# A state-space layer and a mixture of experts in one kernel: a scan started from zero, earlier weight scales, and group 0's pieces placed anew

## The chip, the cores and the metric

The kernel runs on one core of a Trainium2 chip. Its engines are PE (TensorE, matrix products; its weight loads are PEld), DVE (VectorE), ACT (ScalarE), POOL (GpSimd) and SP, which issues the DMA transfers. Each engine runs its own list of instructions in order, and they wait for each other through semaphores. The metric is the time of one execution on the device in microseconds (us); shorter is better. Times inside an execution are in us from its first instruction.

## The reference

Two layers, each followed by a residual and a layer norm, on x of 2 x 2048 tokens with 256 features. Cut to what matters:

```python
# layer 1: a recurrence over time, 128 states
xB = einsum('bsd,nd->bsn', x, B)
state = tanh(state @ A.T + xb_t)              # one token after another, from zero
out = states @ C.T + D * x
x = layernorm(x + layernorm(out + x) * gamma + beta)
# layer 2: 8 experts, 2 chosen per token, and a shared one
scores = sigmoid(x @ router_weight.T)
# the better of two groups of 4 experts by the sum of its top two, then the top two in it
comb = chosen scores / their sum
y = sum_e comb[:, e] * (silu(x @ w_gate[e]) * (x @ w_up[e])) @ w_down[e]
x = layernorm(x + y + (silu(x @ sw_gate) * (x @ sw_up)) @ sw_down)
```

## The kernel before

**Tiling.** The 4096 tokens are 128 runs of L = 32 consecutive tokens, one run on each partition. Tile l is the l-th token of all runs. x is loaded in eight chunks of four tiles (chunk 7 first, then 0 to 6), transposed on PE in 32 halves (`turn_x`), and kept in xT.

**The scan** treats the 128 runs side by side, so that one step is one tile: PE adds the product of x (`drive`, L295) and of the state before (L301), ACT takes the tanh (L526). A run's first state is the last of the run in front of it, which isn't known at first. So there are three stretches: WARM = 4 steps on the last four tiles from zero, whose end gives the seeds; pass one, 32 steps from these seeds; and pass two, 32 steps from pass one's ends, whose states are kept. Afterwards the check compares pass two's ends with the seeds it started from (L822 to L831). Where they differ by more than 2^-20, all engines take a branch that runs the recurrence token by token and does group 0 again (`again`). Between the steps stand the turns of x, those of C and the router's weights, and two small PE instructions for the weight scales.

**Scales and splits.** Every weight tensor is split into two f16 parts for PE. DVE takes each one's largest absolute value (L635); PE transposes the five maxima (L322), DVE reduces them and puts them on a diagonal (L641, L643), PE spreads them over all partitions (L326), and DVE forms powers of two from them (`scales`, L645 to L660). `split(i)` makes the high part (L666) and the low part (L668) of one tensor: 0 is wg, 1 wu, 2 the router's weights rw, 3 wd, 4 C.

**POOL** adds 1 to D, then computes eight times `skip` (x times D, L941), eight times `residual` (x plus beta, L949), the last two behind the two `rsqrt` of group 0 (L961, L963), and later a difference per expert (L978).

**Group 0's pieces.** Tokens then go through eight groups of four tiles. For a group the nine `piece(e, ...)` of PE, ACT and DVE make what the experts need: e = 0 and 1 the product with C (L344, which needs the buffer that DVE's L709 reads), layer norms on DVE (L694 to L734), e = 4 and 5 the transposition of x2 (L359), e = 6 the router's product (L370), e = 7 the tanh of the routing scores (L516), then `choose` and `weigh` on DVE (L759 to L805). Group 0's pieces stand inside pass two, at the steps that the tables `PE_AT` and `ACT_AT` name: `{10: (1, 0)}` puts the first half of piece 1 behind step 10. From step `UP_FROM` on, two of the 24 products of experts 0 and 1 (`early_up`, L382) follow each step, the rest follow the scan. Then comes the check, and then the transposition of group 0's weights (`turn_comb(0)`, L446), with which the groups begin. In a group, PE does the up products of one expert, the down products (L452) of the one before and one piece of the next group.

All order is the order in which the code is written; no scheduler moves anything.

## Time and profile before

| | us |
|---|---|
| Median of three runs | 414.31 (412.38 to 414.62) |
| The profiled execution | 412.55 |
| its span, first to last instruction | 410.8 |
| PE busy | 378.9 (92%) |
| DVE busy | 320.2 (78%) |
| POOL busy | 157.2 (38%) |
| ACT busy | 138.0 (34%) |
| Mean granted clock of TensorE | 0.98 of full |

The profile's page gives the busy time of each engine over the whole span and in 40 slices; the slices of PE read 9 or 8 almost throughout, with a 6 at the start and a gap at about 50 us, while DVE's are low in the first 40 us. Such shares mix stages, so the stages are read one by one: the windows give busy times and the granted clock of a stretch, the timelines list an engine's instructions in order of time with the idle time before each and what ended it.

### The profile page before, as it was taken

Reading aid. Unit: us, or ns where it says so; the run is one execution under the profiler, and the core shown is the slowest. Engines: PE = TensorE matmul, PEld = TensorE weight load, DVE = VectorE, ACT = ScalarE, POOL = GpSimd, SP = SyncE. Lnnn points to the kernel's source line nnn. Section 1 sums busy time; section 2 is a strip of 40 time slices with the busy share of each in tenths; the row PEclk is TensorE's granted clock in tenths of the full one; section 3 lists DMA queues with packets and bytes.
Section 4 is the critical chain, followed back from the end, with each engine's and each line's share of the span. In section 5 each row is a group of like instructions: output and inputs, shape, how many; then the busy total and the mean of one; then the engine's idle time right before and its main releaser. Section 6 shows DMA issues by size and latency. Waiting matters only on the chain.

```text
span 410.8 us, 7488 instructions
## 1 busy us (share of the span) xinstructions
PE 378.9 (92%) x2587; PEld 252.9 (62%) x2587; DVE 320.2 (78%) x744; ACT 138.0 (34%) x280; POOL 157.2 (38%) x149
## 2 busy tenths in 40 slices
PE   6999969859999999998999899989998999999991
PEld 5998868525566656665666566556665665555561
DVE  2343988757976999699969997999799789974564
ACT  2554213222243333432342324232424333333330
POOL 1969515013332443344234423451354125423232
PEclk9999989979999999999999999999999999999997
DMA  7970000005202801270123015501540173005211
GB/s 224 329 273 2 2 0 1 2 4 158 49 0 59 150 2 53 76 131 1 53 90 118 0 53 116 89 0 51 124 82 0 53 145 62 20 34 161 45 53 51
DMA packets 15901, 29.95 MB, mean 73 GB/s; under 512 B 1720, under 2 KB 4288, under 8 KB 15872
## 3 DMA queue, kind: packets, MB, share of 16 engines
q1 hardware_dynamic: 15872, 29.58, 27.6%
q8 instruction: 17, 0.28, 0.3%
q14 instruction: 12, 0.10, 0.1%
HBM read 25.24 MB, written 4.33 MB: 72 GB/s over the span
## 4 chain that ended last, share of the span: by engine, by line
issue 27%; DVE 24%; PE 22%; POOL 12%; DMA 7%; SPq 5%; ACT 2%; POOLq 1%; DVEq 0%; ACTq 0%
PE bank L382 9%; POOL h L978 9%; PE bank L452 4%; DMA xT<-comb_dram 3%; DVE st L694 3%; PE bank L295 3%; DVE xT L850 3%; SPq L208 3%; DVE xT L854 3%; POOL rstd L963 2%; PE bank L301 2%; DMA xres<-in_L_attn_x_dram 2%; DVE wu L725 2%; DMA comb_dram<-combT 1%; DVE wg L734 1%
## 5 line engine op out<-in xcount | busy, mean ns | idle before, releaser
L978 POOL TENSOR_TENSOR h<-xT,h 128x512 f16<-128x512 f32 x72 | 86.1, 1196 | 200.6 <-ACT h L579 200.6
L452 PE MATMUL bank<-wd,h 128*128 128x256 f16 x864 | 106.1, 273 | 0.9 <-DVE wd L862 0.4
L382 PE MATMUL bank<-x2T,wg 128*128 128x512 f16 x432 | 106.3, 382 | 0.0
L382 PE MATMUL bank<-x2T,wu 128*128 128x512 f16 x432 | 105.2, 380 | 0.0
L452 PEld LDWEIGHTS bank<-wd,h 128*128 128x128 f16 x864 | 84.2, 98 | 25.0 <-issue 1.6
L579 ACT ACTIVATE h<-xT 128x512 f16<-128x512 f32 x72 | 45.3, 630 | 131.8 <-DVE xT L854 128.4
L382 PEld LDWEIGHTS bank<-x2T,wu 128*128 128x128 f16 x432 | 42.3, 98 | 51.5 <-issue 0.8
L850 DVE SCALAR_TENSOR_TENSOR xT<-bank,u_un,xT 128x512 f32<-128x512 f32 x64 | 47.6, 744 | 22.5 <-ACT xT L568 21.6
L568 ACT ACTIVATE xT<-bank,g_un 128x512 f32<-128x512 f32 x72 | 49.2, 683 | 46.7 <-PE bank L382 36.5
L382 PEld LDWEIGHTS bank<-x2T,wg 128*128 128x128 f16 x432 | 41.9, 98 | 36.7 <-issue 1.4
L854 DVE TENSOR_TENSOR xT<-xT 128x512 f32<-128x512 f32 x64 | 44.3, 692 | 6.8 <-DMA xT<-comb_dram 4.9
L295 PE MATMUL bank<-xT,BT 128*128 128x128 f32 x272 | 43.6, 285 | 0.0
L295 PEld LDWEIGHTS bank<-xT,BT 128*128 128x128 f32 x272 | 37.5, 200 | 0.1
L963 POOL TENSOR_TENSOR rstd<-rstd,neghalf 128x4 f32<-128x4 f32 (+1 forms) x25 | 25.6, 1022 | 2.0
L694 DVE BATCH_NORM_STATS2 st<-wu 128x6 f32<-128x256 f32 x64 | 23.3, 416 | 0.8
L725 DVE SCALAR_TENSOR_TENSOR wu<-wu,rstd,xres 128x256 f32<-128x256 f32 x32 | 21.7, 740 | 0.5 <-POOL rstd L963 0.5
L734 DVE TENSOR_SCALAR wg<-wu,mv,rstd 128x256 f32<-128x256 f32 x32 | 19.7, 678 | 1.7 <-POOL rstd L963 1.4
L961 POOL TENSOR_TENSOR rstd<-mv,eps 128x4 f32<-128x4 f32 (+1 forms) x25 | 6.9, 274 | 35.7 <-DVE mv L699 35.7
L941 POOL TENSOR_TENSOR xskip<-xres,D_bc 128x1024 f32<-128x1024 f32 x8 | 18.7, 2364 | 3.9 <-DMA xres<-in_L_attn_x_dram 3.8
L359 PE MATMUL bank<-ident,wg 128*128 128x128 f32 x64 | 10.8, 287 | 8.6 <-DVE x2T L740 5.4
L949 POOL TENSOR_TENSOR xres<-xres,beta_bc 128x1024 f32<-128x1024 f32 x8 | 18.6, 2354 | 0.0
L526 ACT ACTIVATE states<-bank 128x128 f32<-128x128 f32 x32 | 8.9, 277 | 24.8 <-PE bank L301 24.8
(122 smaller groups left out, 352.1 us busy)
## 6 DMA issues: line engine op xcount, KB each, us to landing
xT<-comb_dram SPq DMA_DIRECT2D x64, 256.0 KB, 7.4
xres<-in_L_attn_x_dram SPq DMA_DIRECT2D x7, 512.0 KB, 6.0
out_dram<-xskip SPq DMA_DIRECT2D x7, 512.0 KB, 2.7
wd<-in_L_ffn_w_down_dram SPq DMA_DIRECT2D x1, 1024.0 KB, 6.9
xres<-in_L_attn_x_dram SPq DMA_DIRECT2D x2, 256.0 KB, 3.0
out_dram<-xskip SPq DMA_DIRECT2D x2, 256.0 KB, 2.0
B_sb<-in_L_attn_B_dram SPq DMA_DIRECT2D x1, 128.0 KB, 2.6
C_sb<-in_L_attn_C_dram SPq DMA_DIRECT2D x1, 128.0 KB
```

The costliest lines, as they stand in the source:

```text
L295: pe.matmul(ps_scan[s % 2][:, 0:P], BT[:, k, :], xT[:, k, tile, :], start=(k == 0), stop=False)
L382: last = pe.matmul(ps[:, :], w[:, pw, e, m // 3, :], x2T[:, par, px, m // 3, :], start=(m == 0), stop=(m == NUP // 2 - 1))
L452: return pe.matmul(ps_y[t // 2][:, (t % 2) * DM:(t % 2 + 1) * DM], h16[:, e % 3, ph, t * P:(t + 1) * P], wd16[:, pw, e, :], start=start, s ...
L568: nc.scalar.activation(sg[:, b, :], ps_g[b][:, :], ACT.Silu, scale=g_un[:, 0:1]).then_inc(silu_done, 1)
L579: nc.scalar.activation(h16[:, e % 3, 0, :], h[:, b, :], ACT.Copy).then_inc(h_high, 1)
L694: nc.vector.bn_stats(st[:, k, t, :], src(t)).then_inc(st_sem, 1)
L725: nc.vector.scalar_tensor_tensor(y1[:, t, :], y1[:, t, :], rstd[:, 0, 1, t:t + 1], xres[:, g * T4 + t, :], ALU.mult, ALU.add).then_inc(sem ...
L734: nc.vector.tensor_scalar(x2[:, par, t, :], y1[:, t, :], mv[:, 1, t, 0:1], rstd[:, 1, 1, t:t + 1], ALU.subtract, ALU.mult).then_inc(sems[" ...
L850: nc.vector.scalar_tensor_tensor(gu[:, b, :], ps_u[b][:, :], u_un[:, 0:1], sg[:, b, :], ALU.mult, ALU.mult).then_inc(gu_done, 1)
L854: nc.vector.tensor_tensor(h[:, b, :], comb_all[:, e - 1, :], gu[:, b, :], ALU.mult).then_inc(h_done, 1)
L963: nc.gpsimd.tensor_tensor(rstd[:, k, 1, t0:t1], rstd[:, k, 0, t0:t1], neghalf[:, t0:t1], ALU.pow).then_inc(ready, 1)
L978: nc.gpsimd.tensor_tensor(h16[:, e % 3, 1, :], h[:, b, :], h16[:, e % 3, 0, :], ALU.subtract).then_inc(h_low, 1)
```

## The change

- `WARM` is 0: no steps on the last four tiles; pass one starts from zero. The chunks are loaded and used in the order 0 to 7. The steps of the turns of x keep their numbers.
- The scales' two PE instructions stand behind steps 21 and 23 of pass one rather than 26 and 28 behind the warm steps. On DVE the diagonal is made by one instruction with the lower bound 2^-60 in it (a second 5x5 tensor, `tiny_diag`, is made at the start), and the powers come straight from PE's result: one instruction less.
- POOL waits for the ninth step of the scales ahead of `skip(6)`.
- `split(3)` (wd) stands with the other splits, ahead of group 0's first piece.
- Group 0's pieces stand at other steps of pass two, and the early products begin at step 30.
- The check stands ahead of `choose(0)` and `weigh(0)` on DVE; PE's transposition for it stands between the products of expert 0 and of expert 1.

```diff
-    WARM = 4
+    WARM = 0
-        chunks = [L // T4 - 1] + list(range(L // T4 - 1))
+        chunks = list(range(L // T4))
-        PE_AT = {1: (0, 0), 2: (0, 1), 10: (1, 0), 11: (1, 1), 26: (4, 0), 27: (4, 1), 28: (5, 0), 29: (5, 1),
-                 30: (6, 0), 31: (6, 1)}
-        ACT_AT = {27: 5, 29: 6, 31: 7}
-        UP_FROM = 31
+        PE_AT = {1: (0, 0), 2: (0, 1), 8: (1, 0), 9: (1, 1), 23: (4, 0), 24: (4, 1), 26: (5, 0), 27: (5, 1),
+                 29: (6, 0), 30: (6, 1)}
+        ACT_AT = {25: 5, 28: 6, 31: 7}
+        UP_FROM = 30
...
-                if s == WARM + 26:
+                if s == 21:
...
-                if s == WARM + 28:
+                if s == 23:
...
             for n in range(n_up, 2 * NUP):
+                if n == NUP:
+
+                    pe.wait_ge(main["th_done"], 1)
+                    pe.wait_ge(met_part, 1)
+                    pe.transpose(ps_misc[0:1, 0:P], met_row[:, 0:1], ident[:, :]).then_inc(met_all, 1)
                 early_up(n)
-
-
-            pe.wait_ge(met_part, 1)
-            pe.transpose(ps_misc[0:1, 0:P], met_row[:, 0:1], ident[:, :]).then_inc(met_all, 1)
...
+            nc.vector.tensor_scalar(tiny_diag[:, :], ident[0:5, 0:5], 2.0 ** -60, None, ALU.mult).then_inc(tiny_made, 1)
+            dve.wait_ge(tiny_made, 1)
...
-                nc.vector.tensor_scalar(wmax_diag[:, :], ident[0:5, 0:5], wmax_row[:, 0:1], None, ALU.mult).then_inc(wmax_step, 1)
+                nc.vector.scalar_tensor_tensor(wmax_diag[:, :], ident[0:5, 0:5], wmax_row[:, 0:1], tiny_diag[:, :],
+                                               ALU.mult, ALU.max).then_inc(wmax_step, 1)
                 dve.wait_ge(wmax_known, 1)
-                nc.vector.tensor_scalar(wpow[:, :], ps_mats[0][:, P:P + 5], 2.0 ** -60, None, ALU.max).then_inc(wstep, 1)
-                dve.wait_ge(wstep, 1)
-                nc.vector.tensor_scalar(wpow[:, :].bitcast(I32), wpow[:, :].bitcast(I32), 0x7F800000, None,
-                                        ALU.bitwise_and).then_inc(wstep, 1)
+                nc.vector.tensor_scalar(wpow[:, :].bitcast(I32), ps_mats[0][:, P:P + 5].bitcast(I32), 0x7F800000, None,
+                                        ALU.bitwise_and).then_inc(wstep, 2)
...
-            for i in (0, 1, 2):
+            for i in (0, 1, 2, 3):
                 split(i)
...
-            dve.wait_ge(weights_ready, 3)
+            dve.wait_ge(weights_ready, 4)
             for e in range(E1):
                 piece(e, 0, 0, main)
                 if e == 4:
                     split(4)
-                elif e == 6:
-                    split(3)
-            choose(0, main)
-            weigh(0, main)
...
             with dve.If(runs_met == 0):
                 for e in range(E1):
                     piece(e, 0, 0, again)
-                choose(0, again)
-                weigh(0, again)
+                dve.wait_ge(again["th_done"], 1)
+            choose(0, main)
+            weigh(0, main)
...
             for n in range(L // T4):
+                if n == L // T4 - 2:
+
+                    pool.wait_ge(wstep, 9)
                 skip(n)
```

Lines below L256 move by one to four: L295, L301, L344, L359 and L382 become L296, L302, L345, L360 and L383, L446 becomes L448; on DVE L666, L668, L709, L725, L734 and L759 become L670, L672, L713, L729, L738 and L763; on POOL L941 and L949 become L940 and L948.

On POOL, the instructions from the fifth `skip` to group 0's first rsqrt, before and then after, each with its semaphores:

```order
L941 TENSOR_TENSOR xskip<-xres,D_bc 128x1024 [waits x_in4]
L941 TENSOR_TENSOR xskip<-xres,D_bc 128x1024 [waits x_in5]
L941 TENSOR_TENSOR xskip<-xres,D_bc 128x1024 [waits x_in6]
L949 TENSOR_TENSOR xres<-xres,beta_bc 128x1024 [waits xT_turned,skip_done,vecs_in]
L949 TENSOR_TENSOR xres<-xres,beta_bc 128x1024 [waits xT_turned,skip_done] x5
L961 TENSOR_TENSOR rstd<-mv,eps 128x4 [waits mv1_done]
```

```order
L940 TENSOR_TENSOR xskip<-xres,D_bc 128x1024 [waits x_in5]
L940 TENSOR_TENSOR xskip<-xres,D_bc 128x1024 [waits x_in6,wstep]
L940 TENSOR_TENSOR xskip<-xres,D_bc 128x1024 [waits x_in7]
L948 TENSOR_TENSOR xres<-xres,beta_bc 128x1024 [waits xT_turned,skip_done,vecs_in]
L948 TENSOR_TENSOR xres<-xres,beta_bc 128x1024 [waits xT_turned,skip_done] x5
L963 TENSOR_TENSOR rstd<-mv,eps 128x4 [waits mv1_done]
```

The order is the same; the last two skips and the six residuals now stand behind a wait for DVE's scales (`wstep`).

On DVE, from the last instruction of the scales to group 0's first layer norm, before and then after:

```order
L660 TENSOR_SCALAR y_un<-y_un,wpow 128x1
L666 TENSOR_SCALAR wg<-wg,wscale 128x2304
L668 SCALAR_TENSOR_TENSOR wg<-wg,wscale 128x2304
L666 TENSOR_SCALAR wu<-wu,wscale 128x2304
L668 SCALAR_TENSOR_TENSOR wu<-wu,wscale 128x2304
L666 TENSOR_SCALAR rw<-rwT,wscale 128x16
L668 SCALAR_TENSOR_TENSOR rw<-rwT,wscale,rw 128x16
L709 TENSOR_TENSOR wu<-bank,xskip 128x512
```

```order
L664 TENSOR_SCALAR y_un<-y_un,wpow 128x1
L670 TENSOR_SCALAR wg<-wg,wscale 128x2304
L672 SCALAR_TENSOR_TENSOR wg<-wg,wscale 128x2304
L670 TENSOR_SCALAR wu<-wu,wscale 128x2304
L672 SCALAR_TENSOR_TENSOR wu<-wu,wscale 128x2304
L670 TENSOR_SCALAR rw<-rwT,wscale 128x16
L672 SCALAR_TENSOR_TENSOR rw<-rwT,wscale,rw 128x16
L670 TENSOR_SCALAR wd<-wd,wscale 128x2304
L672 SCALAR_TENSOR_TENSOR wd<-wd,wscale 128x2304
L713 TENSOR_TENSOR wu<-bank,xskip 128x512
```

The two parts of wd now stand between the splits and the first y1.

On PE, the end of pass two (the router's product, the last step, the early products, the check), before and then after:

```order
L370 MATMUL bank<-rw,x2T 128x8 x12
L301 MATMUL bank<-states,AT 128x128
L370 MATMUL bank<-rw,x2T 128x8 x12
L382 MATMUL bank<-x2T,wg 128x512 x6
L382 MATMUL bank<-x2T,wu 128x512 x6
L382 MATMUL bank<-x2T,wg 128x512 x6
L382 MATMUL bank<-x2T,wu 128x512 x6
L420 MATMUL bank<-ident,met_row 1x128
```

```order
L371 MATMUL bank<-rw,x2T 128x8 x12
L383 MATMUL bank<-x2T,wg 128x512 x2
L302 MATMUL bank<-states,AT 128x128
L383 MATMUL bank<-x2T,wg 128x512 x4
L383 MATMUL bank<-x2T,wu 128x512 x6
L421 MATMUL bank<-ident,met_row 1x128
L383 MATMUL bank<-x2T,wg 128x512 x6
L383 MATMUL bank<-x2T,wu 128x512 x6
```

Two products come ahead of the last step, and the check's transposition comes ahead of expert 1's twelve products.

## Rows read from the trace of the kernel before

**Rows 1.** Windows: stretch, its length, then busy us (instructions) of each engine.

```profile
core 0: us, PE busy (x) PEld busy (x) DVE busy (x) ACT busy (x) POOL busy (x), PEclk, DMA share, GB/s
56.00:60.00 4.00, 4.00 (x19) 3.77 (x20) 3.17 (x10) 0.56 (x2) 0.00 (x0) 0.59 0.00 0
...
83.50:89.00 5.50, 0.58 (x3) 0.30 (x4) 3.12 (x12) 0.69 (x1) 0.00 (x0) 0.86 0.00 0
...
130.00:170.00 40.00, 38.75 (x266) 23.91 (x265) 35.73 (x88) 13.73 (x23) 14.74 (x15) 1.00 0.33 67
```

**Rows 2.** Timeline of PE: start, us, what, count, idle before and its end.

```profile
28.17 0.44 PE L283 MATMUL bank<-ident,xres 128*128 128x128 f32 x2 [0.71 <-DMA xres<-in_L_attn_x_dram]
28.44 0.39 PE L301 MATMUL bank<-run_state,AT 128*128 128x128 f32 x2
...
29.33 0.39 PE L301 MATMUL bank<-run_state,AT 128*128 128x128 f32 x2
...
39.90 0.38 PE L326 MATMUL bank<-wmax_diag,ones 5*128 5x5 f32 x2 [0.92 <-DVE wmax_diag L643]
...
42.77 0.49 PE L301 MATMUL bank<-seed,AT 128*128 128x128 f32 x2
...
43.62 0.49 PE L301 MATMUL bank<-states,AT 128*128 128x128 f32 x2
```

**Rows 3.** Timeline of DVE, from the last maximum to group 0's first y1.

```profile
26.88 2.55 DVE L635 TENSOR_REDUCE wmax<-wd 128x1 f32<-128x2304 f32 x1 [2.15 <-DMA wd<-in_L_ffn_sw_down_dram]
...
37.72 2.12 DVE L643 TENSOR_SCALAR wmax_diag<-ident,wmax_row 5x5 f32<-5x5 f32 x1
...
42.19 2.28 DVE L651 TENSOR_SCALAR wscale<-wpow 128x5 int32<-128x5 int32 x1
...
45.11 2.87 DVE L666 TENSOR_SCALAR wg<-wg,wscale 128x2304 f16<-128x2304 f32 x1
48.01 2.62 DVE L668 SCALAR_TENSOR_TENSOR wg<-wg,wscale 128x2304 f16<-128x2304 f32 x1
...
55.13 0.69 DVE L709 TENSOR_TENSOR wu<-bank,xskip 128x512 f32<-128x512 f32 x1
```

**Rows 4.** Timeline of POOL, from the last skips to group 0's first rsqrt.

```profile
28.19 4.69 POOL L941 TENSOR_TENSOR xskip<-xres,D_bc 128x1024 f32<-128x1024 f32 x2 [2.29 <-DMA xres<-in_L_attn_x_dram]
32.83 13.93 POOL L949 TENSOR_TENSOR xres<-xres,beta_bc 128x1024 f32<-128x1024 f32 x6
60.35 0.20 POOL L961 TENSOR_TENSOR rstd<-mv,eps 128x4 f32<-128x4 f32 x1 [13.60 <-DVE mv L699]
...
61.71 2.35 POOL L949 TENSOR_TENSOR xres<-xres,beta_bc 128x1024 f32<-128x1024 f32 x1
```

**Rows 5.** Line L725: ns min/median/max, first and last start; whole span, then 182.3:185.2.

```profile
L725 DVE SCALAR_TENSOR_TENSOR wu<-wu,rstd,xres x32: 472/478/2577, 61.8 to 343.7; 128x256 f32<-128x256 f32 x32
...
L725 DVE SCALAR_TENSOR_TENSOR wu<-wu,rstd,xres x4: 477/478/1377, 182.3 to 183.5; 128x256 f32<-128x256 f32 x4
```

**Rows 6.** Timeline of PE in pass two and at its end.

```profile
55.87 0.70 PE L344 MATMUL bank<-CT,states 128*128 128x256 f32 x2 [3.12 <-DVE wu L709]
...
71.63 0.44 PE L359 MATMUL bank<-ident,wg 128*128 128x128 f32 x2
...
77.42 0.47 PE L301 MATMUL bank<-states,AT 128*128 128x128 f32 x2
...
88.69 1.02 PE L446 MATMUL bank<-ident,comb 128*8 128x128 f32 x4 [1.85 <-issue]
```

**Rows 7.** Timeline of DVE: second y1, choice, check.

```profile
58.51 0.69 DVE L709 TENSOR_TENSOR wu<-bank,xskip 128x512 f32<-128x512 f32 x1 [0.71 <-PE bank L344]
...
80.94 0.17 DVE L759 TENSOR_SCALAR score<-th 128x32 f32<-128x32 f32 x1
...
85.90 0.29 DVE L822 TENSOR_TENSOR met_diff<-states,seed 128x126 f32<-128x126 f32 x1
...
87.19 0.14 DVE L831 TENSOR_SCALAR met<-met_top 1x1 int32<-1x1 f32 x1
```

**Rows 8.** The chain of waits, one piece of a group: start, us, what.

```profile
114.99 2.59 PE bank L382 x12
```

More of the change, by code:

```diff
@@ L84, in ssm_moe_kernel @@
         wmax_diag = sb("wmax_diag", [5, 5])
+        tiny_diag = sb("tiny_diag", [5, 5])
         ones = sb("ones", [5, P])
@@ L142, in ssm_moe_kernel @@
         wmax_part, wmax_turned, wmax_step, wmax_known = sem("wmax_part"), sem("wmax_turned"), sem("wmax_step"), sem("wmax_known")
-        wstep, weights_ready = sem("wstep"), sem("weights_ready")
+        wstep, weights_ready, tiny_made = sem("wstep"), sem("weights_ready"), sem("tiny_made")
         w_high = [sem(f"w_high{i}") for i in range(5)]
@@ L316, in _ @@
                     turn_x(FIRST + s // 2, s % 2)
-                if s == WARM:
+                if s == 4:
                     turn_Cr()
-                if s == WARM + 26:
+                if s == 21:
                     pe.wait_ge(wmax_part, 5)
                     pe.transpose(ps_mats[0][0:5, 0:P], wmax[:, :], ident[:, :]).then_inc(wmax_turned, 1)
-                if s == WARM + 28:
+                if s == 23:
                     pe.wait_ge(wmax_step, 3)
@@ L438, in _ @@
                     up_products(e, 0, e).then_inc(again_up, 1)
-                pe.wait_ge(again["route_step"], STEPS)
+                pe.wait_ge(again["th_done"], 1)
             def turn_comb(g):
@@ L619, in _ @@
             dve.wait_ge(AB_turned, 1)
+            dve.wait_ge(consts, 1)
             nc.vector.tensor_copy(AT[:, :], ps_mats[0][:, 0:P])
             nc.vector.tensor_copy(BT[:, :, :].rearrange("p k n -> p (k n)"), ps_mats[0][:, P:(KT + 1) * P]).then_inc(AB_done, 1)
+            nc.vector.tensor_scalar(tiny_diag[:, :], ident[0:5, 0:5], 2.0 ** -60, None, ALU.mult).then_inc(tiny_made, 1)
+            dve.wait_ge(tiny_made, 1)
             UN = 2.0 ** -WTOP / XS
```

## Prediction

> **What bounds the kernel now.** I read the stage windows first, then PE's and DVE's timelines of the first 90 us, then POOL's. From 89 us on the token groups run one after another and PE is busy 38.8 of 40 us [rows 1]; nothing in that part is edited and it has no slack in which a later start could vanish. So the whole question is when the first group may start: PE's transposition of the routing weights (L446) at 88.69 [rows 6]. Ahead of it lies one chain with four links: the scan on PE in steps of 0.85 us; the weight scales and splits on DVE; group 0's y1, layer norms and x2 on DVE with POOL's rsqrt; and the tail (products, check of the runs, choice).
>
> Two places show where PE stands for DVE. At 55.87 L344 had idled 3.12 us for y1 of L709 [rows 6], which had itself to wait for the splits that began at 45.11 and ended shortly before 55.13 [rows 3]. And the scales began only at 37.7 [rows 3] because their transposition stood at step 30 of the scan.
>
> One resource matters more than PE: POOL and DVE exclude each other for certain instructions. L643, a product of 5x5 numbers, took 2.12 us, and L651, one on 128x5, took 2.28 [rows 3], while POOL ran its six residual additions of 2.32 us each (13.93 for six) [rows 4]; both end where one of POOL's ends. L725 takes 0.48, but 2.58 where POOL's L949 had begun 0.05 ahead of it [rows 4, 5]. In a row of four L725 with one POOL instruction due in the middle (182.3 to 183.5), three took 0.48 and one 1.38 [rows 5]: POOL got in between two VectorE instructions that stood back to back. And L651 was served between two of POOL's six, which stood back to back too. So they take turns, one instruction each.
>
> **The change part by part.**
>
> *Four warm steps go.* Pass one is 32 steps in place of 36. The 28 halves of turned x stay, so the four that go are plain ones: 4 x 0.85 = 3.4 us (43.62 - 42.77) [rows 2]. The wait for x at 28.17 (0.71 us, for the load) [rows 2] stays where it is, since turns and loads keep their numbers; it also swallows the new 5x5 instruction tiny_diag, about 0.2 us early on DVE.
>
> *The scales come forward.* Step 21 stands at 28.44 and step 22 at 29.33 (0.89 with a turn) [rows 2]. The reduction of wd ends at 26.88 + 2.55 = 29.43 [rows 3], so the transposition of wmax runs at 29.5 with almost no wait. It pushes step 22 back by 0.3, so step 23 starts at 29.6 + 0.9 = 30.5, and the product with ones follows its turn at 31.4. L643's successor has then run, on an idle POOL, in about 0.2 us in place of 2.12, so the wait of 0.92 ahead of L326 [rows 2] goes as well. Product 0.4, wpow and wscale 0.2 each, the six short ones 0.64 (from 44.47, where L651 ends, to 45.11) [rows 3]: the splits begin at about 32.9, which is 12.2 us earlier. States' first step comes 3.4 + 0.9 - 0.3 = 4.0 us earlier, at 38.8 for 42.77.
>
> *POOL's wait, and what is queued behind it.* POOL now waits for the ninth step of the scales ahead of skip 6. Behind that wait stand skip 6, skip 7 and residuals 0 to 5: eight instructions of 2.32 us, in the trace from 28.19 to 46.76 [rows 4], where they were nearly done when the first split began; only that split paid (2.87, 1.22 of it after POOL's end) [rows 3]. Now all eight start with the splits. The splits are eight as well: high and low parts of wg, wu, rw and wd (wd moves here from behind x2). Taking turns, DVE first: 1.42 for the first; then seven turns of POOL at 2.25 (2.32, less some overlap as in L725, which ended 0.28 after POOL's 64.06 though it takes 0.48) = 15.8; between them three low parts at 2.62 [rows 3] less 0.19 = 7.3, two high parts at 1.22 = 2.4, and twice rw at 0.05. Sum 27.0: the first y1 (L713, before L709) stands at 59.9, against 55.13, that is **+4.8**. Both ends: if POOL comes first, one more turn, +7.1; if rw's two small ones slip past POOL, +0.3, but POOL then still has two instructions left and its rsqrt is late instead (62 to 63.5 for 60.35, no less than +1.7) [rows 4]. An exclusive port makes that floor whatever the order: 11.3 + 8 x 2.2 us of work after 32.9.
>
> No row shows the low part's form (two inputs of 2304 columns, out in f16) beside a running POOL. L725, also scalar_tensor_tensor with two inputs in SBUF, is the nearest; I take its behaviour.
> The Trainium skill, SBUF — State Buffer, section Who interferes with whom, says that a VectorE instruction with two SBUF inputs contends with a GpSimd instruction that reads SBUF, and that whichever comes second blocks in full. By that rule the low parts block too and the sum stands; without it the sum would be the first rival's.
>
> *PE's pieces.* Piece (1,0) moves from step 10 to step 8. PE reaches it at 38.8 + 8 x 0.855 + 0.5 for two pieces + 0.6 = 46.8 and then idles until 60.6: **nearly 14 us in place of 3.1**. The scan, queued behind it, idles too. The clock was at 0.59 of full between 56 and 60 [rows 1], a few us behind that pause, and back after 60; behind the longer one it is low from the restart: the second half of y1 comes 0.6 later (58.51 + 5.4 = 63.9) [rows 7]. From there to x2 the chain on DVE and POOL is untouched, with its two residuals in the same places: first transposition of x2 at 71.63 + 5.4 = 77.0 [rows 6]. PE, from step 9 at 61.2, reaches step 23 at about 76, so DVE is the later one.
>
> *The new places* put (4,0) at step 23, not 26. After it PE runs eight scan steps where it ran five: 5.8 us before (77.42 - 71.63) [rows 6], now 8 x 0.86 + four pieces x 0.25 + about 0.4 of waits = 8.2. Step 31 at 85.2, which is **+7.8**.
>
> *The tail.* Before: 77.42 to 88.69 = 11.3. There split 3 (4.0), then choice and weights (80.94 to 85.90 = 4.96) ran ahead of the check on DVE, and the check ended at 87.33 [rows 7]; all engines went on about 1.0 (PE 1.35) later. Now split 3 is gone from it. Behind step 31 PE issues ten products at 0.216 (2.59 for twelve) [rows 8], turns the check's row at 87.6, DVE ends it at 88.4, branches (1.0), and only then runs the choice: 89.4 + 4.96 = 94.4. PE's remaining twelve products (until 90.4) and its own branch lie under that. L446's successor starts at 94.5: the tail is 9.3, **-2.0**. DVE's met instructions no longer queue behind the choice, but the choice queues behind the branch.
>
> *Sum.* 94.5 - 88.7 = +5.8. One term works back: before, the clock was low in part of 83.5 to 89 (0.86) and beyond 89 [rows 1], with PE at work. Now PE pauses 4 us rather than 5.5, so the low stretch should be shorter: I take -1.0, ends 0 and -2. Result **+4.8 us**. The profiled execution took 412.55 (span 410.8), so 417.3; the three runs' median, 414.31, is 1.8 above it, and on that scale it is **419.1**.
>
> **Rivals.**
> 1. *The low parts don't need the shared port* (faster). For: no row shows them held. Against: L725 was held. Then the high parts and rw's pay perhaps 4 us, y1 stands at 49 to 50 and POOL's queue ends at about 56.5 rather than 62. The rsqrt comes 3.9 us earlier than 60.35, x2 at 67.7, PE reaches step 23 at about 65. With the same last stretch (+2.4) and tail (-2.0) the group starts 3.5 earlier, with the clock 4.5: 408.0, or 409.8 on the median's scale. The point from which it decides is POOL's rsqrt: with it at 61 the change breaks even, ahead of 59 it shows as faster.
> 2. *The port doesn't bind at all in this stretch.* POOL done at 51.8, splits at 45.5, then PE is the bound: about -9, 405.3. Against it stand the rows above.
> 3. *Turns less bad* (small change): POOL's turns overlap more and the floor of +1.7 holds, with the clock's -2: 412.5 to 414.5 on the median's scale, which is measured as no change.
> 4. *The runs don't meet.* Starting from zero, pass one's ends differ more from pass two's, and above 2^-20 all 2048 steps are run one by one, over 1700 us more at 0.85 each. With the reference's inputs the largest difference I work out in single precision is 6.0e-7 from zero and 5.7e-7 with the warm steps, against 9.5e-7: it holds, but by the chip's tanh and rounding, which no row shows.
>
> **How the numbers follow.** Forecast (turns, +2.5 to +8) 0.78; rival 1 0.12; rival 2 0.03; rival 3 0.05; rival 4 0.02. What a measurement of this kernel can tell from no change is about 0.5%, 2.1 us, so 412.2 to 416.4 counts as the same; 0.03 of the forecast's low end falls in it. Faster 0.15, same 0.05 + 0.03 = 0.08, slower 0.75 + 0.02 = 0.77. With the bounds named above (+1.7 to +8.2 around +4.8) the forecast's own range is 416.0 to 422.5; the low end goes down to 412.5 for rival 3, and 0.17 is left out.
>
> **What would show it.** Splits start near 33 and take about 27 us, with four or more of the eight far above their 1.4 and 2.6; POOL's eight end near 62; L345 of piece (1,0) idles over 10 us; L820 starts near 86 and the choice near 89.4; the routing weights are turned near 94.5; from there groups of 40 us as before. Wrong if L672 takes 2.6 beside a running POOL (rival 1), if PE isn't held at step 8 (rival 2), or if the rest isn't a plain shift.

## The result, and the profile after

| | before | after |
|---|---|---|
| Median, us | 413.94 (412.38 to 414.62, 4 runs) | 422.1 (421.21 to 423.26, 4 runs) |
| The profiled execution, us | 412.55 | 421.21 |
| its span, us | 410.8 | 419.5 |
| Mean granted clock | 0.980 | 0.967 |

The ratio is 1.0204, with a 95% interval of 1.0165 to 1.0243: the change makes the kernel 8.2 us slower. The profiled executions differ by 8.66 us, so they show the same thing.

**Where the 8.7 us arise.** First DVE's timeline of after, from the last maximum to the second half of y1 (start, us, instruction; idle time before it and what ended it at the end). It answers to [rows 3] and the first of [rows 7]:

```profile
27.44 2.56 DVE L640 TENSOR_REDUCE wmax<-wd 128x1 f32<-128x2304 f32 x1 [2.07 <-DMA wd<-in_L_ffn_sw_down_dram]
...
30.68 0.21 DVE L648 SCALAR_TENSOR_TENSOR wmax_diag<-ident,wmax_row,tiny_diag 5x5 f32<-5x5 f32 x1
...
33.55 3.63 DVE L670 TENSOR_SCALAR wg<-wg,wscale 128x2304 f16<-128x2304 f32 x1
37.22 4.59 DVE L672 SCALAR_TENSOR_TENSOR wg<-wg,wscale 128x2304 f16<-128x2304 f32 x1
41.73 3.51 DVE L670 TENSOR_SCALAR wu<-wu,wscale 128x2304 f16<-128x2304 f32 x1
45.28 4.59 DVE L672 SCALAR_TENSOR_TENSOR wu<-wu,wscale 128x2304 f16<-128x2304 f32 x1
49.79 2.30 DVE L670 TENSOR_SCALAR rw<-rwT,wscale 128x16 f16<-128x16 f32 x1
52.13 2.26 DVE L672 SCALAR_TENSOR_TENSOR rw<-rwT,wscale,rw 128x16 f16<-128x16 f32 x1
54.32 3.56 DVE L670 TENSOR_SCALAR wd<-wd,wscale 128x2304 f16<-128x2304 f32 x1
57.91 4.57 DVE L672 SCALAR_TENSOR_TENSOR wd<-wd,wscale 128x2304 f16<-128x2304 f32 x1
62.57 0.69 DVE L713 TENSOR_TENSOR wu<-bank,xskip 128x512 f32<-128x512 f32 x1
...
66.72 0.69 DVE L713 TENSOR_TENSOR wu<-bank,xskip 128x512 f32<-128x512 f32 x1 [1.46 <-PE bank L345]
```

And POOL's timeline of the same stretch, which answers to [rows 4]:

```profile
33.60 5.80 POOL L940 TENSOR_TENSOR xskip<-xres,D_bc 128x1024 f32<-128x1024 f32 x2 [7.05 <-PE bank L284]
39.35 20.71 POOL L948 TENSOR_TENSOR xres<-xres,beta_bc 128x1024 f32<-128x1024 f32 x6
68.56 0.20 POOL L963 TENSOR_TENSOR rstd<-mv,eps 128x4 f32<-128x4 f32 x1 [8.49 <-DVE mv L703]
...
69.92 2.35 POOL L948 TENSOR_TENSOR xres<-xres,beta_bc 128x1024 f32<-128x1024 f32 x1
```

The two must be read side by side. The splits begin at 33.55, 11.6 us earlier than before. But each of the eight split instructions is about 2.0 to 2.2 us longer than alone, even the two that handle only 16 columns, and they reach from 33.55 to 62.5, which is 28.9 us. POOL's six residuals take 20.71 for 13.93 before. Taken one by one, the two engines' instructions end in turn: POOL at 35.96, DVE at 37.18, POOL at 39.39, DVE at 41.81, and so on until POOL at 60.07 and DVE at 62.48. Neither list shows idle time in this stretch: an instruction that is held by the other engine shows as a long one. So y1 comes 7.4 us later (62.57 for 55.13), although the splits began 11.6 earlier.

PE's timeline of after, second pass to the first group, answers to [rows 6]:

```profile
63.32 1.22 PE L345 MATMUL bank<-CT,states 128*128 128x256 f32 x2 [15.68 <-DVE wu L713]
...
79.82 0.44 PE L360 MATMUL bank<-ident,wg 128*128 128x128 f32 x2 [0.93 <-DVE wg L738]
...
87.88 0.38 PE L302 MATMUL bank<-states,AT 128*128 128x128 f32 x2
...
97.23 1.02 PE L448 MATMUL bank<-ident,comb 128*8 128x128 f32 x4 [4.10 <-DVE comb L809]
```

One pause of 15.68 us stands in the place of the 3.12 [rows 6]. The first transposition of x2 is 8.2 us late, step 31 10.5, and the group's weights 8.5 (97.23 for 88.69).

The windows of after (length, busy time of each engine, granted clock), as [rows 1]:

```profile
50.00:56.00 6.00, 0.00 (x0) 0.00 (x0) 5.96 (x3) 0.00 (x0) 6.00 (x3) 0.57 0.00 0
56.00:60.00 4.00, 0.00 (x0) 0.00 (x0) 3.96 (x2) 0.00 (x0) 4.00 (x2) 0.50 0.00 0
60.00:68.00 8.00, 4.68 (x18) 4.33 (x19) 6.30 (x12) 0.55 (x2) 0.07 (x1) 0.51 0.01 2
68.00:76.00 8.00, 8.00 (x59) 7.00 (x58) 6.89 (x19) 2.57 (x10) 3.88 (x5) 1.00 0.00 1
...
95.00:102.00 7.00, 4.77 (x14) 2.60 (x15) 4.58 (x16) 1.68 (x3) 1.15 (x1) 0.51 0.06 19
...
138.60:178.60 40.00, 38.63 (x265) 23.78 (x264) 35.70 (x88) 13.67 (x23) 14.63 (x15) 1.00 0.34 67
```

In the first two PE does nothing and DVE and POOL both look fully busy; that pair is the sign of the fault. The last line is the steady state, with 38.63 busy us of 40 for 38.75 before: from the first group on everything is shifted by 8.5 to 8.7 us.

### The profile page after: what moved, and what is told of

Its sections match the earlier page's. It is cut to its first block, busy times and chain, and to the rows that moved or that the text cites. A ratio compares the mean times of both kernels' runs of the same rounds, so it can differ in the third digit from the quotient of the medians.

```text
span 419.5 us, 7440 instructions
## 1 busy us (share of the span) xinstructions
PE 376.7 (90%) x2563; PEld 250.4 (60%) x2563; DVE 329.8 (79%) x744; ACT 136.7 (33%) x276; POOL 164.9 (39%) x149
## 4 chain that ended last, share of the span: by engine, by line
DVE 28%; issue 26%; PE 18%; POOL 13%; DMA 7%; SPq 5%; ACT 2%; POOLq 1%; DVEq 0%; ACTq 0%
PE bank L383 10%; POOL h L980 9%; PE bank L454 4%; DVE st L698 4%; DMA xT<-comb_dram 3%; POOL rstd L965 3%; SPq L209 3%; DVE xT L849 3%; DVE wu L729 3%; DVE xT L853 3%; DVE wg L738 2%; DMA xres<-in_L_attn_x_dram 2%; DMA comb_dram<-combT 1%; DVE wu L672 1%; DVE wg L672 1%
## 5 line engine op out<-in xcount | busy, mean ns | idle before, releaser
L383 PE MATMUL bank<-x2T,wg 128*128 128x512 f16 x432 | 106.2, 382 | 0.0
L383 PE MATMUL bank<-x2T,wu 128*128 128x512 f16 x432 | 105.0, 379 | 0.0
L383 PEld LDWEIGHTS bank<-x2T,wu 128*128 128x128 f16 x432 | 42.3, 98 | 51.1 <-issue 0.3
L849 DVE SCALAR_TENSOR_TENSOR xT<-bank,u_un,xT 128x512 f32<-128x512 f32 x64 | 47.6, 744 | 22.5 <-ACT xT L570 21.6
L383 PEld LDWEIGHTS bank<-x2T,wg 128*128 128x128 f16 x432 | 42.0, 98 | 36.3 <-issue 1.4
L296 PE MATMUL bank<-xT,BT 128*128 128x128 f32 x256 | 41.1, 285 | 0.0
L296 PEld LDWEIGHTS bank<-xT,BT 128*128 128x128 f32 x256 | 35.5, 201 | 0.0
L948 POOL TENSOR_TENSOR xres<-xres,beta_bc 128x1024 f32<-128x1024 f32 x8 | 25.4, 3198 | 0.0
L940 POOL TENSOR_TENSOR xskip<-xres,D_bc 128x1024 f32<-128x1024 f32 x8 | 19.8, 2510 | 7.6 <-PE bank L284 7.0
L729 DVE SCALAR_TENSOR_TENSOR wu<-wu,rstd,xres 128x256 f32<-128x256 f32 x32 | 21.7, 739 | 0.5 <-POOL rstd L965 0.5
L738 DVE TENSOR_SCALAR wg<-wu,mv,rstd 128x256 f32<-128x256 f32 x32 | 19.7, 678 | 1.7 <-POOL rstd L965 1.4
L345 PE MATMUL bank<-CT,states 128*128 128x256 f32 x16 | 6.4, 517 | 15.7 <-DVE wu L713 15.7
L360 PE MATMUL bank<-ident,wg 128*128 128x128 f32 x64 | 10.8, 287 | 9.5 <-DVE x2T L744 5.0
```

Source lines behind the costliest of these rows:

```text
L296: pe.matmul(ps_scan[s % 2][:, 0:P], BT[:, k, :], xT[:, k, tile, :], start=(k == 0), stop=False)
L383: last = pe.matmul(ps[:, :], w[:, pw, e, m // 3, :], x2T[:, par, px, m // 3, :], start=(m == 0), stop=(m == NUP // 2 - 1))
L729: nc.vector.scalar_tensor_tensor(y1[:, t, :], y1[:, t, :], rstd[:, 0, 1, t:t + 1], xres[:, g * T4 + t, :], ALU.mult, ALU.add).then_inc(sem ...
L738: nc.vector.tensor_scalar(x2[:, par, t, :], y1[:, t, :], mv[:, 1, t, 0:1], rstd[:, 1, 1, t:t + 1], ALU.subtract, ALU.mult).then_inc(sems[" ...
L849: nc.vector.scalar_tensor_tensor(gu[:, b, :], ps_u[b][:, :], u_un[:, 0:1], sg[:, b, :], ALU.mult, ALU.mult).then_inc(gu_done, 1)
```

## Experiments

In the expectations, "the eight" are skips 6 and 7 and residuals 0 to 5. Theory A: the loss is the meeting of the eight splits with these eight at the port. Theory B: the loss comes from another part, namely the check ahead of the choice or the new places.

### Undoing single parts

**e2_no_wait**: after, without POOL's wait.

```diff
             for n in range(L // T4):
-                if n == L // T4 - 2:
-
-                    pool.wait_ge(wstep, 9)
                 skip(n)
```

> The changed kernel without POOL's wait for the ninth step of the scales. Theory: skip 6, skip 7 and one residual run from 28.7 on, ahead of the splits; the scales end some 0.7 us later, five of POOL's turns stand among the splits instead of eight, first y1 at 58 for 62.6, device time 417.5 (416 to 419). If the wait shields the scales by more than it costs the splits: 422 or more. Rivals A and B: no change from 422.

Measured: 417.56 us (416.97 to 417.95), ratio 1.010 (1.0063 to 1.0138). As expected: 4.5 us better than after and still 4.4 slower than before. Without the wait POOL's two skips are done when the splits begin, and only six residuals meet them (five were expected; the first of the six had already begun, and the first split took 2.87 rather than 3.63). The two parts of wd then run unheld (1.41 and 2.62), and y1 stands at 58.71 in place of 62.57:

```profile
56.01 2.62 DVE L672 SCALAR_TENSOR_TENSOR wd<-wd,wscale 128x2304 f16<-128x2304 f32 x1
58.71 0.69 DVE L713 TENSOR_TENSOR wu<-bank,xskip 128x512 f32<-128x512 f32 x1
```

**b2_wait**: the kernel before, with this wait alone.

```diff
             for n in range(L // T4):
+                if n == L // T4 - 2:
+
+                    pool.wait_ge(wstep, 9)
                 skip(n)
```

> The kernel before with nothing but POOL's wait for the ninth step of the scales ahead of skip 6. Theory: scales 4.6 us earlier (splits from 40.5), but then eight of POOL's turns stand among six splits: first y1 at 61.5 for 55.1, device time 421 (419 to 422). If the wait by itself helps by keeping POOL off the scales: 409 to 411.

Measured: 420.29 us (419.97 to 421.92), ratio 1.0177 (1.0131 to 1.0223), as expected. One wait on an engine that is busy 38% of the time costs 6.4 us. DVE's timeline of this kernel:

```profile
41.13 3.61 DVE L666 TENSOR_SCALAR wg<-wg,wscale 128x2304 f16<-128x2304 f32 x1
44.78 4.59 DVE L668 SCALAR_TENSOR_TENSOR wg<-wg,wscale 128x2304 f16<-128x2304 f32 x1
...
57.33 2.30 DVE L666 TENSOR_SCALAR rw<-rwT,wscale 128x16 f16<-128x16 f32 x1
```

and POOL's:

```profile
41.18 5.78 POOL L941 TENSOR_TENSOR xskip<-xres,D_bc 128x1024 f32<-128x1024 f32 x2 [14.57 <-DVE y_un L660]
46.92 19.79 POOL L949 TENSOR_TENSOR xres<-xres,beta_bc 128x1024 f32<-128x1024 f32 x6
```

The scales end at 41.1 in this kernel, since the wait frees them from POOL too. The pattern is that of after, to 0.02 us: 3.61, 4.59, 2.30. Six splits pay six turns; y1 stands at 62.03 for 55.13 before.

**e3_wd_split_back**: after, with the split of wd where it stood.

```diff
-            for i in (0, 1, 2, 3):
+            for i in (0, 1, 2):
                 split(i)
...
-            dve.wait_ge(weights_ready, 4)
+            dve.wait_ge(weights_ready, 3)
...
                     split(4)
+                elif e == 6:
+                    split(3)
```

> The changed kernel with the split of wd back behind piece 6 of group 0. Theory: six splits stand among POOL's eight instead of eight, first y1 at 54 to 55 for 62.6; POOL's eight end at 60 to 61 instead, and the rsqrt at 60.5 for 68.6; device time 413.5 to 415. Rivals A and B: 421 to 422, or more by the 4 us of the split in the tail.

Measured: 415.81 us (414.36 to 417.23), ratio 1.0058 (1.0036 to 1.008), the direction as expected, and the time 0.8 us above the expected range. Between the other splits and y1 wd's two parts cost 8.1 us (3.56 and 4.57 above); in their old place they cost 4.0 (1.41 at 78.87, 2.62 at 80.31), since POOL is quiet there. The same two instructions on the same engine cost twice as much where POOL is busy.

**e4_old_places**: after, with the old tables.

```diff
-        PE_AT = {1: (0, 0), 2: (0, 1), 8: (1, 0), 9: (1, 1), 23: (4, 0), 24: (4, 1), 26: (5, 0), 27: (5, 1),
-                 29: (6, 0), 30: (6, 1)}
-        ACT_AT = {25: 5, 28: 6, 31: 7}
-        UP_FROM = 30
+        PE_AT = {1: (0, 0), 2: (0, 1), 10: (1, 0), 11: (1, 1), 26: (4, 0), 27: (4, 1), 28: (5, 0), 29: (5, 1),
+                 30: (6, 0), 31: (6, 1)}
+        ACT_AT = {27: 5, 29: 6, 31: 7}
+        UP_FROM = 31
```

> The changed kernel with the old tables of places (piece 1 at steps 10 and 11, piece 4 at 26 and 27, piece 5 at 28, 29, piece 6 at 30, 31, early products from 31). Theory: first y1 stays at 62.6, PE idles 14 us instead of 15.7, five steps instead of eight follow the first transposition of x2: device time 420 (419.5 to 421). Rival A (the places are the cause): back to about 414.

Measured: 420.12 us (419.38 to 422.15), ratio 1.0176 (1.0129 to 1.0223), as expected. With x2 late on DVE either way (the first L360 at 79.83 for 79.82) the new places only put more steps behind it: the group's weights are turned at 95.78 rather than 97.23. The 2.0 us between the medians are no more than a hint by themselves, since the intervals of e4 and after overlap; the 1.45 us of the traces point the same way.

**e5_check_last**: after, with the check back behind the choice and its transposition behind all early products.

```diff
             for n in range(n_up, 2 * NUP):
-                if n == NUP:
-
-                    pe.wait_ge(main["th_done"], 1)
-                    pe.wait_ge(met_part, 1)
-                    pe.transpose(ps_misc[0:1, 0:P], met_row[:, 0:1], ident[:, :]).then_inc(met_all, 1)
                 early_up(n)
+            pe.wait_ge(met_part, 1)
+            pe.transpose(ps_misc[0:1, 0:P], met_row[:, 0:1], ident[:, :]).then_inc(met_all, 1)
...
+            choose(0, main)
+            weigh(0, main)
             dve.wait_ge(scan_tanh, WARM + 2 * L)
...
-            choose(0, main)
-            weigh(0, main)
...
```

> The changed kernel with the check back behind the choice of group 0 on DVE, and its transposition back behind all early products on PE. Theory (the tail got shorter by the split of wd that left it, not by the new order): choice from 89 to 94, check known at 95.4, routing weights turned at 96.7 for 97.2; device time 421.5, within 0.3% of the changed kernel. Rival B (the new order lengthens the tail): 2 us or more faster. If the new order is what shortened the tail: 424.

Measured: 421.61 us (420.72 to 422.46), ratio 1.0205 (1.0157 to 1.0252): the same as after, as expected. From the first transposition of x2 to the turning of the weights it is 16.8 us here and 17.4 in after, so the new order of check and choice gains nothing. Together e4 and e5 leave of theory B only the up to 2.0 us of the places. That these too arise only because x2 is late is argued and not shown: no run has the old places with everything else new and POOL's work out of the way.

### Moving POOL's work

**e1_pool_late**: after, without the wait; of the eight only residuals 0 and 1 stay early, the other work stands behind group 0's second rsqrt.

```diff
-            for n in range(L // T4):
-                if n == L // T4 - 2:
-
-                    pool.wait_ge(wstep, 9)
+            for n in range(L // T4 - 2):
                 skip(n)
-            for n in range(L // T4 - 2):
+            for n in range(2):
                 residual(n)
...
-            residual(L // T4 - 2)
             rsqrt(1, 0, main["mv2_done"], rstd_step, main["rstd2_ready"], 1)
-            residual(L // T4 - 1)
+            for n in (L // T4 - 2, L // T4 - 1):
+                skip(n)
+            for n in range(2, L // T4):
+                residual(n)
```

> The changed kernel, but POOL runs skip 0 to 5 and residual 0 and 1, and the other eight instructions (skip 6, 7, residual 2 to 7) only behind group 0's second rsqrt; no wait for the scales. Theory (turns at the shared port, eight of POOL's among eight splits): splits from 33.6 to 46 in place of 33.6 to 62.6, PE is not held at step 8 (15.7 us of idle gone), the routing weights are turned at 81 to 84 for 97.2, device time 406 to 410, faster than both kernels. Rival A (the new places of the pieces hold PE, whatever the port does): the places are the same, so 419 or more. Rival B (the choice behind the check makes the tail longer): tail the same, so 419 or more.

Measured: 414.01 us (412.07 to 415.51), ratio 1.0014 (0.9991 to 1.0038): 8 us better than after, but no better than before. The expectation was missed. DVE's timeline shows both halves of the answer:

```profile
34.95 1.42 DVE L670 TENSOR_SCALAR wg<-wg,wscale 128x2304 f16<-128x2304 f32 x1
36.41 2.62 DVE L672 SCALAR_TENSOR_TENSOR wg<-wg,wscale 128x2304 f16<-128x2304 f32 x1
...
47.50 0.69 DVE L713 TENSOR_TENSOR wu<-bank,xskip 128x512 f32<-128x512 f32 x1
...
58.29 9.49 DVE L738 TENSOR_SCALAR wg<-wu,mv,rstd 128x256 f32<-128x256 f32 x4 [1.41 <-POOL rstd L962]
67.70 2.42 DVE L670 TENSOR_SCALAR C<-CT,wscale 128x256 f16<-128x256 f32 x1
70.16 2.45 DVE L672 SCALAR_TENSOR_TENSOR C<-CT,wscale,C 128x256 f16<-128x256 f32 x1
```

PE's shows who pays:

```profile
48.25 0.70 PE L345 MATMUL bank<-CT,states 128*128 128x256 f32 x2 [0.58 <-DVE wu L713]
...
73.26 0.69 PE L360 MATMUL bank<-ident,wg 128*128 128x128 f32 x2 [7.28 <-DVE x2T L744]
```

The splits run unheld, y1 comes 15.1 us earlier than in after, and PE's wait of 15.68 shrinks to 0.58. So the first half of theory A stands. But the moved instructions begin at 58.22, beside the layer norm of x2 and the split of C: four L738 take 9.49 us and the two splits of C 2.42 and 2.45. The run below has 1.38, 0.35 and 0.48 for them. The meetings were not removed but handed to other instructions on the same chain. My mistake was to ask only whether POOL's work was off the splits, not what it would meet instead.

**f1_spread**: after, without the wait. All skips run at once; residual 0 stands behind the splits, 1 to 5 behind the split of C, 6 and 7 in groups 0 and 1. DVE waits for what it needs only.

```diff
-            dve.wait_ge(res_done, 2)
+            dve.wait_ge(skip_done, 1)
...
+                if e == 3:
+                    dve.wait_ge(res_done, 1)
                 piece(e, 0, 0, main)
...
-            dve.wait_ge(res_done, L // T4)
+            dve.wait_ge(res_done, L // T4 - 2)
             group(0, 0, first=True)
             group(1, 1)
+            dve.wait_ge(res_done, L // T4)
...
-                if n == L // T4 - 2:
-
-                    pool.wait_ge(wstep, 9)
...
-            for n in range(L // T4 - 2):
-                residual(n)
...
+            pool.wait_ge(weights_ready, 4)
+            residual(0)
             rsqrt(0, 0, main["mv1_done"], rstd_step, main["rstd1_ready"], 0)
-            residual(L // T4 - 2)
             rsqrt(1, 0, main["mv2_done"], rstd_step, main["rstd2_ready"], 1)
-            residual(L // T4 - 1)
+            pool.wait_ge(weights_ready, 5)
+            for n in range(1, L // T4 - 2):
+                residual(n)
...
                     low(g, e, (par + e) % 2)
+                    if e == 0 and isinstance(g, int) and g < 2:
+                        residual(L // T4 - 2 + g)
```

> The changed kernel with POOL's work taken out of the way of the instructions that need the shared port: all eight skips at once (no wait for the scales), residual 0 behind the splits, residuals 1 to 5 behind the split of C, residuals 6 and 7 in groups 0 and 1. Theory: splits from 34.3 to about 47 without turns, step 8 held under 1 us, x2 ready before PE reaches step 23, so that the scan on PE bounds this part; routing weights turned at 79 to 81 for 97.2; device time 404.5 (403 to 407). Rival A (places) and rival B (choice behind the check): at best the 414 of the kernel before.

Measured: 405.68 us (404.55 to 406.12), ratio 0.9817 (0.977 to 0.9863): as expected, and faster than both kernels. DVE's timeline has the same instructions as those of e1 and after:

```profile
35.40 1.42 DVE L670 TENSOR_SCALAR wg<-wg,wscale 128x2304 f16<-128x2304 f32 x1
...
47.94 0.69 DVE L713 TENSOR_TENSOR wu<-bank,xskip 128x512 f32<-128x512 f32 x1
48.67 0.75 DVE L698 BATCH_NORM_STATS2 st<-wu 128x6 f32<-128x256 f32 x2
...
49.74 1.29 DVE L722 SCALAR_TENSOR_TENSOR wu<-wu,mv,gamma_bc 128x256 f32<-128x256 f32 x2
...
59.18 1.38 DVE L738 TENSOR_SCALAR wg<-wu,mv,rstd 128x256 f32<-128x256 f32 x4 [1.40 <-POOL rstd L963]
60.48 0.35 DVE L670 TENSOR_SCALAR C<-CT,wscale 128x256 f16<-128x256 f32 x1
...
70.85 2.33 DVE L822 TENSOR_TENSOR met_diff<-states,seed 128x126 f32<-128x126 f32 x1 [2.58 <-ACT states L528]
```

PE reaches the second half of y1 and x2's first transposition (48.78 and 62.11) without a wait and turns the group's weights at 80.61, 16.6 us earlier than after and 8.1 earlier than before. One meeting is left on the chain: the check's difference takes 2.33 in place of 0.29, beside residual 5. Groups 0 and 1, with residuals 6 and 7 in them, take 1.2 us longer than before (78.3 from the first turning of weights to the third, for 77.2).

**b3_spread**: the kernel before, with the same spreading (residuals 0 and 1 behind the splits, since before used chunk 7 first). Shown is POOL's part; DVE's waits and the two residuals in the groups change as in f1.

```diff
...
-            for n in range(L // T4 - 2):
-                residual(n)
...
+            pool.wait_ge(weights_ready, 3)
+            residual(0)
+            residual(1)
             rsqrt(0, 0, main["mv1_done"], rstd_step, main["rstd1_ready"], 0)
-            residual(L // T4 - 2)
             rsqrt(1, 0, main["mv2_done"], rstd_step, main["rstd2_ready"], 1)
-            residual(L // T4 - 1)
+            pool.wait_ge(weights_ready, 4)
+            for n in range(2, L // T4 - 2):
+                residual(n)
...
```

> The kernel before (warm steps, old places, old order of the check) with the same spreading of POOL's residuals. Theory: scales no longer delayed by POOL, splits from 40.5 to 49, step 10 not held, routing weights turned at 83 to 84 for 88.7: device time 408 (407 to 410). What is between this and f1 is the worth of the rest of the change: about 3.5 to 4 us. If the port mattered only in the changed kernel: 413.

Measured: 411.39 us (410.2 to 412.2), ratio 0.9949 (0.9925 to 0.9973). The direction is right, the size is not. DVE's timeline:

```profile
51.63 3.38 DVE L718 SCALAR_TENSOR_TENSOR wu<-wu,mv,gamma_bc 128x256 f32<-128x256 f32 x2
...
71.77 1.83 DVE L666 TENSOR_SCALAR wd<-wd,wscale 128x2304 f16<-128x2304 f32 x1
73.64 4.59 DVE L668 SCALAR_TENSOR_TENSOR wd<-wd,wscale 128x2304 f16<-128x2304 f32 x1
```

Here residuals 0 and 1 meet a layer norm (3.38 for 0.88) and residuals 2 to 5 (65.41 to 75.8) the split of wd, whose low part stands ahead of the choice. The difference from f1, 5.7 us, is more than the 3.5 to 4 expected, and it holds such meetings. The next pair was made for that.

**f2_later** and **b4_later**: the same two kernels, with the last residuals at places where DVE idles or reads PSUM: 5 behind the check, ahead of group 0; 6 and 7 (in b4: 6 and 0) behind the last difference of groups 0 and 1. b4 has only residual 1 behind the splits, 2 to 4 behind the split of C, and 7 in group 1. The edit of f2 against f1, POOL's part (DVE's waits for the residuals follow it):

```diff
...
-            for n in range(1, L // T4 - 2):
+            for n in range(1, 5):
                 residual(n)
...
+            pool.wait_ge(main["route_step"], STEPS)
+            residual(5)
...
-                    if e == 0 and isinstance(g, int) and g < 2:
-                        residual(L // T4 - 2 + g)
...
+                    elif e == 7 and isinstance(g, int) and g < 2:
+                        pool.wait_ge(main["route_step"], (g + 2) * STEPS)
+                        residual(6 + g)
```

> The kernel of the run f1_spread with residuals 5, 6 and 7 placed anew: 5 behind the check and group 0's weights, 6 and 7 behind the last difference of groups 0 and 1, where DVE reads PSUM or idles. By the theory (only a meeting at the port costs, and only where DVE's instruction is on the chain) two meetings go: met_diff took 2.33 in place of 0.29, of which PE's wait of 0.98 was on the path, so 1.0; and groups 0 and 1 lost about 1.3 beside residuals 6 and 7, of which 1.0 should return. 405.7 - 2.0 = 403.7 us, range 402.8 to 405.0. By the rival (the last three residuals cost the same wherever they stand, since POOL's 2.32 us are always taken from DVE's stretch) 405.7 again.

Measured: 403.84 us (402.4 to 405.55), ratio 0.9774 (0.9748 to 0.9801): as expected, the fastest of all. POOL's timeline shows residual 5 in its new place:

```profile
78.47 2.35 POOL L952 TENSOR_TENSOR xres<-xres,beta_bc 128x1024 f32<-128x1024 f32 x1 [8.77 <-DVE comb L809]
```

and DVE's what it now stands beside, and the check without it:

```profile
69.83 0.29 DVE L822 TENSOR_TENSOR met_diff<-states,seed 128x126 f32<-128x126 f32 x1 [2.59 <-ACT states L528]
...
78.43 0.75 DVE L848 SCALAR_TENSOR_TENSOR xT<-bank,u_un,xT 128x512 f32<-128x512 f32 x1
```

The group's weights are turned at 78.45, on PE:

```profile
78.45 1.01 PE L448 MATMUL bank<-ident,comb 128*8 128x128 f32 x4 [4.10 <-DVE comb L809]
```

That is 10.2 earlier than before; 1.5 of it is lost again in groups 0 to 2, where residuals still meet DVE's products of two SBUF tensors (beside residual 6 one, L855, took 2.16 for 0.69). Of the 2.2 us by which this turning is earlier than in f1, 1.0 is there already at x2's first transposition (61.10 for 62.11), where nothing was edited; the reduction of wd too began 1.0 earlier (27.71 for 28.74), behind its load.

> The kernel before with the same kind of places: only residual 1 behind the splits, 2 to 4 behind the split of C, 5 behind the check, 6 and 0 behind the last difference of groups 0 and 1, 7 in group 1. In b3_spread L718 was held (3.38 in place of 0.88) but PE reached the first transposition of x2 without a wait, so freeing it gives nothing; the split of wd was held by 2.4 us ahead of the choice (1.83 and 4.59 in place of 1.41 and 2.62), of which 2.0 should return since the choice ends the tail there; the groups' loss falls from 2.1 to about 0.7. 411.4 - 3.4 = 408.0 us, range 407.0 to 409.5. The difference from f2_later is then what the rest of the change is worth with no meeting in either: 4.3 us expected (3.5 to 5), against the 5.7 between f1_spread and b3_spread. By the rival as above: 411.4 again, and 5.7 stays.

Measured: 410.67 us (409.97 to 411.35), ratio 0.9943 (0.9922 to 0.9964): missed, by 2.7 us. The first half of the expectation held: the split of wd runs in 1.41 and 2.62, and the weights are turned at 82.77, 3.2 earlier than in b3:

```profile
82.77 1.01 PE L446 MATMUL bank<-ident,comb 128*8 128x128 f32 x4 [1.86 <-issue]
```

The second half failed, in group 1, on DVE:

```profile
126.87 2.70 DVE L856 TENSOR_TENSOR xT<-xT 128x512 f32<-128x512 f32 x1
129.49 1.40 DVE L864 SCALAR_TENSOR_TENSOR wd<-bank,y_un,wg 128x512 f32<-128x512 f32 x2
```

and on PE:

```profile
131.03 1.47 PE L452 MATMUL bank<-wd,h 128*128 128x256 f16 x12 [1.56 <-DVE wd L864]
```

Residual 7 holds a product of two SBUF tensors (2.70 for 0.69), and PE waits 1.56 us for what follows it. Group 1 takes 42.4 us from turning to turning, for 40.4 in f2. PE has hardly any slack in a group [rows 1], so a meeting there is worth no less than one ahead of the groups; I had put it at nearly nothing.

For the question of the pair, the turning of the group's weights is the cleaner measure, since ahead of it, in both, DVE is held on y1's layer norm by 0.4 us only, and PE doesn't wait there: 82.77 against 78.45, that is 4.3 us, as expected. (f2's scales were also held, by 0.8 us in all, 0.46 and 0.73 for 0.21 and 0.17; PE reached y1 without a wait all the same.) This is what the rest of the change (no warm steps, early scales, new places, the split of wd and the check moved) is worth where POOL is out of the way. It is good to about 1 us: the reduction of wd began at 26.84 in b4 and at 27.71 in f2, behind a load that neither edit touches. The medians differ by 6.8, the profiled executions by 6.1. The groups account for 1.7 of that (from the first turning of the weights to the last it is 280.4 us in b4, 278.7 in f2), and 4.3 and 1.7 are the whole 6.1. The last 0.7 is no more than the choice of the execution: the profiled one of b4 is the fastest of its six.

## Why the prediction was right

The forecast was 419.1 (412.5 to 422.5), with 0.77 for slower; measured were 422.1, only 0.4 below the upper end. The mechanism was right: DVE's splits and POOL's eight took turns, and PE stood for it. The size was well short: +4.8 was forecast, +8.2 measured on the medians and +8.66 on the profiled executions. That the time still fell in the range was in part luck: the upper end stood for +8.2, worked out for "POOL comes first" alone, and the +8.66 of the profiled executions lies above it. Step by step:

- **Scales and start of the splits**: 32.9 forecast, 33.55 measured. 0.56 of it is the later load of wd (reduction at 27.44 for 26.88). That isn't the change's doing as far as the runs show: in b2, b3 and b4, whose loads are those of before, the same reduction begins at 27.49, 27.61 and 26.84. The diagonal took 0.21, as forecast.
- **Length of the splits**: 27.0 forecast, 29.0 measured up to the start of y1; this is the largest error. All took turns, the low parts (4.59 for 2.62) and the tiny ones too, so rivals 1 and 2 fell, and with them rival 3. But the working said "Taking turns, DVE first". The first split took 3.63, not 1.42: POOL had the first turn. DVE paid eight turns, not seven. They came to 2.06 each: the eight lengths above sum to 29.01, those of the same instructions in e1 to 12.56, and the difference, 16.45, goes over eight. The bound "if POOL comes first, one more turn, +7.1" was the right one; y1 came 7.4 later. I had no row on who wins when one instruction of DVE releases both, and chose the mild end. The working even had the right length: its floor of 11.3 + 8 x 2.2 is 28.9 us, and the stretch took 28.9, but with POOL first it is DVE that ends last, so the floor held for y1 (POOL's eight ended at 60.07, ahead of the 62 forecast).
- **PE's wait at step 8**: "nearly 14 us" forecast, 15.68 measured, the same error passed on.
- **Second half of y1**: +0.6 forecast for the low clock, +0.8 measured (66.72 to 58.51 is 8.2, against 7.4). From there to x2 nothing changed, as forecast: L360 8.2 later.
- **Step 23 to 31**: 8.2 forecast, 8.06 measured. The **tail**: 9.3 forecast, 9.35 measured, with the choice at 92.24, later than the 89.4 forecast by about the delay of what lies ahead (step 31 at 87.88 for 85.2). In the kernel before, this tail is also PE's thinnest slice ahead of the last one, a 5 at 82 to 92 us, thinner than the 6 at about 50 us.
- **The clock's give-back**: −1.0 forecast, nothing measured; no row had a price for it. The low stretch at the start of group 0 did not get shorter with PE's shorter pause: it is 6.8 us in both traces (87.4 to 94.2 before, 95.2 to 102.0 after), and the groups' shift is 8.5 us at the first turning of weights and 8.7 at the end. Nor would a shorter one have given anything back here: in e2 it is 3.4 us (93.4 to 96.8), and the first group takes 37.1 us from turning to turning, as before and after (37.1 each).

4.8 + 2.0 (POOL first) + 0.6 (load) + 0.2 (second half) + 1.0 (clock) = 8.6, against the 8.66 measured. Rival 4 fell: there is no second run over the 2048 steps in the time.

The page's rule too came out as weighed. The Trainium skill, SBUF — State Buffer, section Who interferes with whom, says that a VectorE instruction with two SBUF inputs contends with a GpSimd instruction that reads SBUF, and the low parts show it: 4.59 beside POOL, 2.62 without.

What was shown: the wait alone costs 6.4 us in the kernel before (b2), taking it away gives 4.5 in after (e2), and with POOL's work spread the rest of the change gains (f2 against b4, 4.3 us at the first turning, to about 1 us). What is only argued: that the new places cost up to 2 us just because x2 is late, and how the 4.3 us divide among the parts of the change; no run takes these apart.

## What to carry to other kernels

When both DVE and POOL are busy at once and instructions are longer than elsewhere, count the meetings: each held DVE instruction costs nearly the whole of a POOL instruction (2.06 of 2.32 us here), and that even for 16 columns. So don't put a wait ahead of POOL's queue that lets it start together with DVE's densest stretch; give each POOL instruction a place of its own, next to idle time of DVE or to work that the traces show unheld, such as the additions that read PSUM and the statistics. One SBUF input alone is no safe sign: the high parts of the splits have just one and were held. Look at what the moved work will meet there and whether PE waits for that: e1 and b4 failed on just this.
